# First attention: fourth weight block ahead of the later inputs, and the statistics of groups 3 and 4 in steps 16 to 25

## The reference

```python
x = x + _L0_attn_ref(_layernorm(x, axis=-1), wq, bq, wk, bk, wv, bv, wo, bo, ln_g, ln_b)

def _L0_attn_ref(h, ...):            # 16 heads of 128
    mu, var = mean(h), mean((h - mu) ** 2)
    x = (h - mu) * rsqrt(var + EPS) * ln_g + ln_b
    q, k, v = x @ wq.T + bq, x @ wk.T + bk, x @ wv.T + bv
    q, k = rope(q), rope(k)
    attn = softmax(where(causal, -inf, q @ k.T / sqrt(128)))
    return (attn @ v) @ wo.T + bo + h
```

## Time and profile before

| | |
|---|---|
| median of 3 runs | 992.02 us (990.56 to 992.89) |
| the profiled execution, its own time | 994.6 us |
| its span, first to last instruction | 992.8 us |
| mean granted TensorE clock | 0.990 of full speed |
| TensorE busy | 936.3 us, 94% |
| VectorE busy | 797.6 us, 80% |
| ScalarE busy | 708.6 us, 71% |
| GpSimd busy | 359.0 us, 36% |
| from steps 0 to 63, until about | 510 us |

### The profile page before, as it was taken

One profiled execution on the slowest core, in us unless ns is written; L12 is line 12 of the kernel. 1 busy time (PEld: TensorE's weight loads), 2 busy tenths in 40 slices (PEclk: granted clock), 3 DMA queues, 4 the chain that ended last, 5 costly groups with the idle time before them and its releaser, 6 DMA issues. The chain is left out here.

```text
span 992.8 us, 19508 instructions
## 1 busy us (share of the span) xinstructions
PE 936.3 (94%) x6591; PEld 778.6 (78%) x6607; DVE 797.6 (80%) x1561; ACT 708.6 (71%) x1970; POOL 359.0 (36%) x323
## 2 busy tenths in 40 slices
PE   8889999999999999999989988889999989999998
PEld 4678888888988988888978866667778789875554
DVE  5999987888888787787857989889999754477885
ACT  5778877878778788777742347598999735448882
POOL 2243333433334333443300120266655310007882
PEclk9999999999999999999999997999999999999999
DMA  7423100000000000201215000000000000008762
GB/s 213 119 67 86 39 24 25 23 23 23 25 23 24 24 23 24 82 23 45 66 21 138 1 1 1 1 2 2 2 3 2 2 2 1 1 27 285 236 223 86
DMA packets 61603, 50.42 MB, mean 51 GB/s; under 512 B 18112, under 2 KB 53056, under 8 KB 61504
## 3 DMA queue, kind: packets, MB, share of 16 engines
q1 hardware_dynamic: 61504, 49.17, 16.8%
HBM read 36.74 MB, written 2.23 MB: 39 GB/s over the span
## 5 line engine op out<-in xcount | busy, mean ns | idle before, releaser
L387 POOL TENSOR_TENSOR roped_q<-roped_q,sin_q 128x512 f32<-128x512 f32 x64 | 81.8, 1279 | 261.8 <-DVE sin_q L569 261.8
L454 ACT ACTIVATE P<-banks,neg_max 128x128 f32<-128x128 f32 x256 | 90.5, 368 | 29.9 <-DVE neg_max L585 29.4
L387 POOL TENSOR_TENSOR roped_k<-roped_k,sin_k 128x512 f32<-128x512 f32 x64 | 83.0, 1297 | 47.6 <-DVE sin_k L569 47.6
L1809 ACT ACTIVATE win_P<-banks,win_neg_max 128x128 f32<-128x128 f32 x256 | 91.2, 382 | 4.9 <-DVE win_neg_max L1896 3.6
L462 ACT ACTIVATE oT_hi<-banks,bv_col 128x512 fp32r<-128x512 f32 x64 | 43.9, 687 | 62.4 <-PE banks L776 60.7
L1742 POOL TENSOR_TENSOR win_P<-win_P,win_inv 128x512 f32<-128x512 f32 x64 | 66.5, 1040 | 53.4 <-DVE win_inv L1901 53.3
L480 ACT ACTIVATE sin_q<-banks 64x512 f32<-64x512 f32 x128 | 76.0, 593 | 3.3 <-PE banks L37 1.1
L480 ACT ACTIVATE sin_k<-banks 64x512 f32<-64x512 f32 x128 | 75.9, 593 | 3.1 <-PE banks L37 0.8
L731 PE MATMUL banks<-WO_lo,oT_hi 128*128 128x256 f32 x256 | 73.3, 286 | 2.3 <-DVE oT_lo L589 2.3
L746 PE MATMUL banks<-roped_k,roped_q 128*128 128x128 f32 x512 | 68.3, 276 | 7.1 <-ACT banks L445 6.9
L568 DVE SCALAR_TENSOR_TENSOR roped_k<-banks,qk_bias,cos 128x512 f32<-128x512 f32 x64 | 48.0, 750 | 30.8 <-ACT sin_k L480 30.5
(11 more groups left out here) (440 smaller groups left out, 3093.6 us busy)
## 6 DMA issues: line engine op xcount, KB each, us to landing
PT<-blocks SPq DMA_DIRECT2D x620, 16.0 KB, 1.8
ret_V<-moe_gate_rows SPq DMA_DIRECT2D x16, 512.0 KB, 5.0
ctx<-moe_gate_rows SPq DMA_DIRECT2D x16, 512.0 KB, 5.2
X<-in_x SPq DMA_DIRECT2D x4, 512.0 KB, 6.9
stage<-in_wqT SPq DMA_DIRECT2D x4, 512.0 KB, 4.1
stage<-in_wvT SPq DMA_DIRECT2D x4, 512.0 KB, 6.5
stage<-in_woT SPq DMA_DIRECT2D x4, 512.0 KB, 5.1
ctx<-in_ctxT SPq DMA_DIRECT2D x4, 512.0 KB, 4.2
```

The source lines that it names most:

```text
L387: nc.gpsimd.tensor_tensor(roped[w][:, p, :], roped[w][:, p, :], sin_part[w][:], ALU.add).then_inc(roped_sum[w], 1)
L454: ins = nc.scalar.activation(P[:, :, i, :], SC[:, i * 128:(i + 1) * 128].rearrange("p (q n) -> p q n", n=Q), ACT.Exp, bias=neg_max[:, u % ...
L1809: ins = nc.scalar.activation(P[:, h % 2, s, i, :], SC[2 * (h % 2) + s][:, i * 128:(i + 1) * 128], ACT.Exp, bias=neg_max[:, h % 2, at:at + ...
```

## The change

1. In SyncE's queue the loads of W3 and W4 go ahead of the loads of X of groups 1 to 3, instead of behind them.
2. The rounding of W3 on ScalarE and its split on VectorE stand in step 0 instead of step 1, at the same place in the step: between V and sin_k, and between `rope` of q and of k.
3. The statistics are taken for one group at a time. Group 1: two `bn_stats` at the end of step 3, two at the end of step 4, the norms at the end of step 5. Group 2: two each at the end of steps 16 and 17, norms in step 18. Group 3: two each at the end of steps 21 and 23, norms in step 25. The powers follow in the same steps on GpSimd. Before, steps 3, 4 and 5 had four `bn_stats` each and step 6 the norms of all 12 batches.

The counts that the semaphores are waited for follow from this. The diff, cut to its core:

```diff
-        LN_PARTS = ((slice(0, GROUP), GROUP), (slice(GROUP, B), B + 8))
+        STATS_AT = {3: (4, 5), 4: (6, 7), HEADS0: (8, 9), HEADS0 + 1: (10, 11), HEADS0 + 5: (12, 13), HEADS0 + 7: (14, 15)}
+        NORMS_AT = {5: 1, HEADS0 + 2: 2, HEADS0 + 9: 3}
+        POWERS_AT = NORMS_AT
+
+        def ln_done(g):
+            return (GROUP + 8) * (g + 1)
...
+                for i in range(STAGES + 1, 5):
+                    load_weights(i)
                 for g in range(1, NG):
                     load_x(g)
-                for i in range(STAGES + 1, 5):
-                    load_weights(i)
...
-                def powers(part):
-                    some, n = LN_PARTS[part]
-                    pool.wait_ge(ln0, n + 8)
+                def powers(g):
+                    some = slice(g * GROUP, (g + 1) * GROUP)
+                    pool.wait_ge(ln0, ln_done(g))
...
-                    if t == 6:
-                        powers(1)
+                    if t in POWERS_AT:
+                        powers(POWERS_AT[t])
...
-                            if s == 1 and w == 0:
+                            if s == 0 and w == 0:
                                 round_weights(STAGES + 1)
...
-                def group_stats(g):
-                    dve.wait_ge(x_loaded[g], 16)
-                    for b in range(g * GROUP, g * GROUP + GROUP):
+                def some_stats(some):
+                    dve.wait_ge(x_loaded[some[0] // GROUP], 16)
+                    for b in some:
                         nc.vector.bn_stats(stats[:, b, :], X[:, b, :]).then_inc(ln0, 1)
 
-                def both_norms(part):
+                def both_norms(g):
-                    some, n = LN_PARTS[part]
+                    some, n = slice(g * GROUP, (g + 1) * GROUP), ln_done(g) - 8
...
                         rope(s, r % 2, r, 0)
-                        if s == 1:
+                        if s == 0:
                             split_weights(STAGES + 1)
                         rope(s, r % 2, r, 1)
                     if g == 0:
-                        if r in (3, 4, 5):
-                            group_stats(r - 2)
-                        if r == 6:
-                            both_norms(1)
                         if r == 12:
                             add_h(0)
+                    if s in STATS_AT:
+                        some_stats(STATS_AT[s])
+                    if s in NORMS_AT:
+                        both_norms(NORMS_AT[s])
```

More of the change, by code:

```diff
@@ L399, in _ @@
                         add_const(t // HEADS0 - 1, t % HEADS0 - 4)
-                    if t == 6:
-                        powers(1)
-                pool.wait_ge(ln0, B + 23)
+                    if t in POWERS_AT:
+                        powers(POWERS_AT[t])
+                pool.wait_ge(ln0, ln_done(NG - 1) + 7)
                 nc.gpsimd.tensor_tensor(rstd[:, 0:NEXT], var_eps[:, 0:NEXT], minus_half[:, 0:NEXT], ALU.pow).then_inc(rstd_ready, 1)
@@ L543, in normalise @@
                 def normalise(b):
-                    dve.wait_ge(rstd_ready, 1 if b < GROUP else 3)
+                    dve.wait_ge(rstd_ready, b // GROUP * 2 + 1)
                     if b >= GROUP:
@@ L550, in add_h @@
                 def add_h(b):
-                    dve.wait_ge(rstd_ready, 2 if b < GROUP else 4)
+                    dve.wait_ge(rstd_ready, b // GROUP * 2 + 2)
                     wait(dve, h_added, 2 * b)
@@ L626, in step @@
                         dve.wait_ge(restated, NEXT)
-                        finish_stats(nc, dve, ln0, B + 16, stats[:, 0:NEXT, :], mean[:, 0:NEXT], var_eps[:, 0:NEXT], ln_tmp[:, :, 0:NEXT], LN_EPS)
+                        finish_stats(nc, dve, ln0, ln_done(NG - 1), stats[:, 0:NEXT, :], mean[:, 0:NEXT], var_eps[:, 0:NEXT], ln_tmp[:, :, 0:NEXT], LN_EPS)
                     if live(u, STEPS):
@@ L660, in drain @@
                     take_ret_V(7)
-                group_stats(0)
+                some_stats(range(GROUP))
                 both_norms(0)
```

## The result

The changed kernel takes 995.13 us (median of 14 executions) against 992.62 of the kernel before beside it: ratio 1.0025 [1.0017, 1.0032], 2.5 us slower. 994.2 against 992.02 had been forecast, 2.2 slower. The profiled execution of after took 995.94 us, span 994.2; that of before 994.6, span 992.8.

The account below looks back on a forecast made before the run. TensorE bounds it from about 130 us, before that often waiting on the loop beside it, which pays for work ending VectorE's step. Front -2.2 plus back +4.4 gave +2.2: 994.2 us against the 992.02 median, range 991.0 to 996.3.

Parts of the forecast that it names:

- rival E: Steps 0 and 1: W3 lands late, step 0 loses what step 1 gains or more; up to +5.0 us; chance 0.08.
- the term -0.3: Step 1: no rounding or split of W3 there, so `rope` of k starts at 25.2 instead of 25.54; gain 0.3 us.
- Step 3 gives nothing: Step 3 drops two `bn_stats` but ScalarE waits there for W7, so no gain; bound 0 to 0.66 us.
- the front: Early steps up to step 7: net gain 2.3 us, taken as 2.2, passed unchanged to step 16.
- Rival D: Step 3 also gives 0.66 as W7 comes earlier, or steps 16 to 25 stop less: +1.5, 993.5 us; chance 0.13.
- Rival C: Steps 5, 18, 25: norms of four columns cost 1.0 us, not 2.01; sum -0.8, 991.2 us; chance 0.13.
- The back: Steps 16 to 26: added statistics and norms stop TensorE for 3.06 us by step 20, 4.4 in all.
- a lead of 1.46: Step 26: score start minus mask start minus 0.73, the loop's slack before TensorE waits; 1.46 us, 0.27 in step 20.
- Rival B: Steps 16 to 25: added work hidden in VectorE's idle time or a lead over 3.3 us; 989.8 us; chance 0.10.
- Rival F: Step 19: TensorE stands for 2 us and its granted clock falls, costing 1.5 once; 995.7 us; chance 0.12.

Follow-up runs that it names:

- e1: Kernel before with only the changed load order and W3's rounding and split in step 0, statistics unmoved; 992.75 us, ratio 0.9997.
- e3: Kernel before with only the statistics moved, W3's loads and split as before; 995.27 us, ratio 1.0021 to the kernel before.
- e5: Changed kernel with all four `bn_stats` of group 1 in step 3, none in step 4; 994.53 us, ratio 1.0017 to the kernel before.
- e7: Changed kernel with only the norms of steps 18 and 25 moved ahead of `scale`; 991.36 us, ratio 0.9988 to the kernel before.
- e4: Changed kernel with statistics and norms of steps 16 to 25 ahead of `scale`, same steps; 991.09 us, ratio 0.9982 to the kernel before.
- e6: Changed kernel, steps 16-25 statistics and norms ahead of `scale`, group 1's `bn_stats` all in step 3, its norms ahead of `scale` in step 6; 989.12 us, ratio 0.9964.

## Why the prediction was right, point by point

**Loads and W3.** Forecast: `rope` of k in step 0 one later, in step 1 0.3 earlier. Measured from an equal start: 1.03 later, and 0.3 earlier (24.84 against 25.54, less 0.39). W3 went out at 11.09, not 12.2, because W0's split, which it waits for, ended earlier. The uncertain landing (rival E) did not come up: no wait ahead of the rounding, and e1 is 0.9997 of before. But the gain of 0.3 is one against a traced execution that had lost the start in step 1. The forecast took the long split of that row, 2.23 us, for the rule. Against an execution like e3's in step 1 the same term is a loss of 0.5. The forecast did not have this: the term -0.3 holds for the trace from which it was read and probably not for the median.

**Step 3 gives nothing, step 4 0.66; in steps 5 and 6 the norms cancel and four `bn_stats` (1.3 us) are left.** The masks after, against before: step 4 -0.70 (as step 3), step 5 -1.36, step 6 -0.73, step 7 -2.74. So 0, 0.66, a loss of 0.63, a gain of 2.01. From an equal start the front is 2.35 at the mask of step 7 (forecast 2.3) and 2.17 at the score of step 16 (forecast 2.2). The zero of step 3 holds only with block moves of 7.0 to 7.2 us, as in before, after and e5; where they took 6.56, 6.68 and 6.70 (e3, e7, e4) the mask of step 4 gained another 0.50 to 0.55 us. e6 had 6.46 with four `bn_stats` in step 3 and gained 0.07. Rival D's first half is thus real in some executions, not in others.

**Three sets of norms are each held by the add.** The mean took 1.15, 1.16 and 1.15 us in steps 5, 18 and 25, and 0.17 in e4, where no add runs beside it. Rival C priced this at 1.0 a set and is refuted. (By its own terms its sum is -3.1 + 2.38 = -0.7, not -0.8, which changes nothing.) The Trainium skill (SBUF — State Buffer, "Who interferes with whom") says that the instruction that comes first gets the shared port for its whole length and the other is blocked. The pairs above agree in both directions: 1.23 beside 2.33, and 2.23 beside 1.28. By the same section two SBUF inputs are enough to be held, and the third instruction of the norms again was not: 0.16 us at 160.93, a hundredth ahead of the add at 160.94. There the trace can't decide.

**The back.** Forecast: TensorE is stopped for 3.06 us by step 20 and 4.4 by step 26. Measured: the score goes from -2.56 in step 16 to +0.12 in step 20 and +1.27 in step 26, stops of 2.68 and 3.83. The mechanism is the one named, the size is 0.57 too high. The working of the forecast was 5.86 on the loop less a lead of 1.46. The loop in fact lost 5.53 (mask -2.80 in step 16, +2.73 in step 26): two sets of norms of 1.93, not 2.01, four pairs of `bn_stats` of 0.64 or 0.65, not 0.66, and 0.90 won back, nearly all in steps 23 and 26, not 0.80. And the lead in step 16 was 0.78 instead of 0.54: the front had moved the masks by 2.80 but the scores by 2.56. The forecast had booked 0.1 of this as lost to TensorE and none of it as cover; 0.24 came back as cover. With the 0.33 that the loop lost less than forecast this makes the 0.57. After step 26 only 0.09 more is lost, `add_out` in step 35 included (+1.27 at step 26, +1.36 at step 27 and at step 35), within the forecast's 0 to 0.3.

**Rival B**, the faster end, had one condition: a lead over 3.3 us, or the work in VectorE's idle time. By step 20 the loop had lost 3.20 and TensorE 2.68, so the lead covered 0.5. That the idle time is real is shown by e4, which puts the work there and is faster than before. Idle share was the wrong thing to read in the earlier trace rows; where in the step it lies is what counts.

**Rival F.** TensorE stood for a microsecond at a time, and the granted clock stayed at 1.00 from 130 to 230 us.

So +2.2 was forecast from -2.2 and +4.4; the traces show -2.17 and +3.92, that is +1.75, and the timed executions +2.5 [1.7, 3.2]. The difference of 0.75 is about the 0.8 us that the traced execution of before lost in step 1. Read so, the front is worth 1.4 us and not 2.2, and the back costs 3.9 and not 4.4. These two misses go in opposite directions, 0.8 and 0.5; that the sum came as close as it did is in part luck. The mechanism, work at the end of VectorE's step against a small lead, was right and is shown by e3, e4 and e7.

## What to carry to other kernels

In a loop over several engines, look for the engine's wait inside its own step and put small work in front of it; work at the end of the step, ahead of the instruction on which the next step hangs, is paid in full even when the engine is idle a sixth of the time. A stage in which TensorE is full is no free place either: measure the lead of the loop that feeds it, and compare it with what is moved there. What is shared out over more places pays its fixed price at each: one set of norms behind a GpSimd add cost 2.0 us for twelve columns, and three sets of four cost 1.9 each.

Before two traces are compared to a microsecond, look for the first place where they part ahead of the change. Here the reference execution had lost 0.8 us there, more than the loads and the place of W3 were worth together.

## What the runs showed of the hardware that had not been expected

A start 0.04 to 0.27 us earlier decides which of a VectorE and a GpSimd instruction takes nearly twice its time: the split 1.23 or 2.09 to 2.23 us, the add 1.28 or 2.3, and a power of 512 elements 1.02 or 2.00 (0.15 us behind a split). A landing 0.2 us earlier was thus worth 0.8 us of the loop in step 1, and executions of the same program up to there fell on both sides.

The same ten block moves held SP's queue for 6.46 to 7.20 us in different executions, and with them the issue of the next weight load.
